# One score run, 64x64 value pieces and a new slot order in a local-attention kernel

## The reference

```python
h = shift_token(x)
q, k, v = split(h @ wqkv)                      # 8 heads of 64
q, k = l2norm(q) * qs, l2norm(k) * ksc
q, k = rotary_xpos(q, k)
sim = einsum('bhwid,bhwjd->bhwij', q * 8, k)   # window 128, keys of this and the previous window
sim = where((i < j) | (i > j + 128) | (j == -1), -max, sim)
out = softmax(sim) @ v
x = x + out @ wo
```

## Time and profile before

| | us |
|---|---|
| median of three runs | 3194.92 |
| lowest, highest | 3190.87, 3195.54 |
| profiled execution, span from first to last instruction | 3193.4 |
| PE busy in it | 3068.6 (96%) |
| DVE, ACT, POOL busy | 2350.6, 1729.0, 1622.9 |

### The profile page before, as it was taken

The page is one execution under the profiler, slowest core; times in us unless marked ns, Lnnn a source line. Parts: engine busy times, 40 slices in busy tenths (PEclk is TensorE's granted clock), DMA queues, the critical chain, the costliest instruction groups (busy, mean ns, idle before and its releaser), DMA issues.

```text
span 3193.4 us, 99022 instructions
## 1 busy us (share of the span) xinstructions
PE 3068.6 (96%) x35586; PEld 2681.3 (84%) x35586; DVE 2350.6 (74%) x6543; ACT 1729.0 (54%) x4532; POOL 1622.9 (51%) x1839
## 2 busy tenths in 40 slices
PE   6999999999999999999899999989999899999889
PEld 5888878878887888998788878878888788888778
DVE  6888767677776787777777767767777688777766
ACT  4767642266767224665667672237767622454445
POOL 7777730177776224333777761037777444317610
PEclk9999999999999999999999999999999999999999
DMA  4211121021111101000211112102111200100001
GB/s 135 67 45 44 37 81 33 23 63 40 36 40 39 42 20 43 11 10 21 58 40 36 40 39 76 30 26 66 37 39 34 72 21 13 27 0 1 1 14 40
DMA packets 178774, 122.82 MB, mean 38 GB/s; under 512 B 27533, under 2 KB 175337, under 8 KB 178025
## 3 DMA queue, kind: packets, MB, share of 16 engines
q1 hardware_dynamic: 177432, 117.77, 13.8%
q10 hardware_dynamic: 1104, 1.90, 0.2%
HBM read 48.29 MB, written 20.98 MB: 22 GB/s over the span
## 4 chain that ended last, share of the span: by engine, by line
PE 87%; DVE 6%; issue 3%; POOL 1%; ACT 1%; DMA 1%; SPq 0%; DVEq 0%; POOLq 0%; ACTq 0%
PE bank L347 15%; PE bank L348 13%; PE bank L349 13%; PE bank L511 8%; PE bank L480 6%; PE bank L452 3%; PE bank L732 2%; PE bank L731 2%; PE bank L730 2%; PE bank L724 2%; PE bank L725 2%; PE bank L489 2%; PE bank L676 2%; PE bank L675 2%; PE bank L490 2%
## 5 line engine op out<-in xcount | busy, mean ns | idle before, releaser
L2652 POOL TENSOR_TENSOR prob<-prob,rsum 128x384 f32<-128x384 f32 x512 | 416.2, 834 | 155.8 <-DVE rsum L1861 155.8
L1209 ACT ACTIVATE prob<-prob,nmax 128x192 f32<-128x192 f32 x1024 | 455.8, 454 | 2.2 <-DVE nmax L1854 2.2
L1401 ACT ACTIVATE gate<-bank,bias 128x512 f32<-128x512 f32 x192 | 132.4, 690 | 512.0 <-PE bank L349 511.9
L2639 POOL TENSOR_TENSOR rn<-ss,mhalf 128x16 f32<-128x16 f32 x128 | 375.9, 2937 | 10.7
L1854 DVE CUSTOM_DVE_ANT_0 prob<-bank,masks,rn 128x192 f32<-128x192 f32 x768 | 275.1, 414 | 100.1 <-PE bank L480 99.3
L2646 POOL TENSOR_TENSOR qk<-rot_t 128x512 f32<-128x512 f32 x256 | 331.9, 1297 | 23.3 <-DVE ss L1828 21.3
L347 PE MATMUL bank<-wqkv_hi,hT_hi 128*128 128x512 f32 x768 | 329.5, 429 | 14.7 <-DVE rot_t L1816 6.1
L2620 POOL TENSOR_TENSOR rstd<-meanvar,eps 128x4 f32<-128x4 f32 x48 | 12.4, 259 | 620.4 <-DVE meanvar L1786 620.4
L348 PE MATMUL bank<-wqkv_lo,hT_hi 128*128 128x512 f32 x768 | 303.0, 395 | 0.0
L349 PE MATMUL bank<-wqkv_hi,hT_lo 128*128 128x512 f32 x768 | 302.8, 394 | 0.0
L347 PE MATMUL bank<-gT_hi,w_hi 128*128 128x512 f32 x704 | 277.2, 394 | 2.6 <-issue 2.6
(11 more groups left out here) (292 smaller groups left out, 9831.1 us busy)
## 6 DMA issues: line engine op xcount, KB each, us to landing
Vlo<-V SPq DMA_DIRECT2D x256, 64.0 KB, 2.0
Vhi<-V SPq DMA_DIRECT2D x256, 64.0 KB, 2.0
H<-Y SPq DMA_DIRECT2D x128, 64.0 KB, 1.8
H<-ya SPq DMA_DIRECT2D x128, 64.0 KB, 1.8
yb<-Y SPq DMA_DIRECT2D x128, 64.0 KB, 1.6
HB<-Y SPq DMA_DIRECT2D x32, 256.0 KB, 2.8
HB<-yb SPq DMA_DIRECT2D x32, 256.0 KB, 3.1
raw<-in_L_ffn_wqkv SPq DMA_DIRECT2D x4, 1536.0 KB, 8.3
```

What stands on the lines that cost most here:

```text
L1209: ins = e.activation(pb, pb, ACT.Exp, bias=nm[r][:, x:x + 1], scale=-1.0, accum_out=sums[r][:, x:x + 1])
L2639: e.tensor_tensor(rn[u][:, :], ss[:, :], mhalf[:, :], ALU.pow).then_inc(s_plRN, 1)
L2652: e.tensor_tensor(pair, pair, rs[:, 2 * gi:2 * gi + 2].unsqueeze(2).to_broadcast([P, 2, KW]), ALU.mult).then_inc(s_plPN[gi], 1)
```

## The change

The banks of PSUM are laid out anew: banks 2 to 4 become one area of 1536 columns in which each head has its 192 columns (SCORE_AT), so that all eight heads' scores of a tile stand there at once; banks 6 and 7 take P times V, heads 0 to 3 in one and 4 to 7 in the other, and the output projection moves to the second half of bank 7. The scores become one run of 32 matmuls with one semaphore at its end, and a wait of PE for a piece of its own in the middle (s_peSB). P times V does the parts with Vlo and Vhi first, with the 64 rows only that belong to the head, as 64x64 pieces, and the parts with V behind them. The turned K and the projected V use bank 5, the turned Q and projected Q bank 0, the turned H and projected K bank 1, the turned P the score banks once they are read. The lists of all four engines are new: the softmax of tile T and its turns (pt_) now lie in slot T, behind its scores. SP's list is the same. The fill (begin) is written out step by step instead of through partial slots, and the drain has one slot less on DVE and ACT.

```diff
+SCORE_AT = (384, 768, 576, 1344, 0, 960, 192, 1152)
+SCORE_ORDER = ((1, 4, 0), (1, 4, 1), (5, 6, 1), (5, 6, 0), (7, 0, 0), (7, 0, 1), (3, 2, 0), (3, 2, 1))
+TURN_BANK = (3, 2, 2, 4)
...
+bank = [ctx.enter_context(nc.psum_tensor(f"bank{i}", [P, 512], F32))[:, :] for i in range(2)]
+scores = ctx.enter_context(nc.psum_tensor("scores", [P, 3 * 512], F32))
+bank += [scores[:, 512 * i:512 * (i + 1)] for i in range(3)]
+bank.append(ctx.enter_context(nc.psum_tensor("bank5", [P, 512], F32))[:, :])
+pair_bank = ctx.enter_context(nc.psum_tensor("pair_bank", [P, 2 * 512], F32))
+bank += [pair_bank[:, 512 * i:512 * (i + 1)] for i in range(2)]
+numerator = pair_bank[:, :].rearrange("p (a c) -> p a c", a=2)[:, :, 0:2 * P]
+projected = bank[7][:, 2 * P:4 * P]
...
+def v_bank(run, T):
+    return bank[0] if run == DEPTH and isinstance(T, int) and T == 0 else bank[5]
+
+def k_turn_bank():
+    return bank[5]
...
         def qk_(T, u, j):
+            early = isinstance(T, int) and T < 3
+            if j == 0 and not early:
+                qT_read(T - 2)
+            elif j == 0 and T == (1 if run == DEPTH else 2):
+                qT_read(0)
+            elif j == 0 and T > 0:
+                q_read(T - 1)
+            elif j == 1 and spare(run, T):
+                k_read(T - 1)
+            proj(bank[j], u, INNER * j, INNER).then_inc(s_peQK[j], 1)
...
         def v_(T, u):
+                if run == DEPTH:
+                    q_read(0)
+            elif isinstance(T, int) and T == 1:
+                kT_read(0)
+            elif isinstance(T, int) and T == 2:
+                v_read(1)
+            else:
+                kT_read(T - 2)
+            proj(v_bank(run, T), u, 2 * INNER, INNER).then_inc(s_peV, 1)
...
         def tr_(T, u, j):
             G = R0 + T
             e.wait_ge(s_plAD[0] if j == 0 else s_dvQN, G + 1 + OFF)
+            if j == 0 and isinstance(T, int) and T == 0 and run == DEPTH:
+                v_read(0)
+            elif j == 0 and inside(T + 1):
+                q_read(T + 1)
+            elif j == 0:
+                qT_read(T - 1)
+            elif isinstance(T, int) and T == 0:
+                v_read(0)
+            elif inside(T + 1):
+                v_read(T + 1)
             else:
+                kT_read(T - 1)
...
+        def sc_(T, u):
             G = R0 + T
             r = u % 2
+            e.wait_ge(s_acKT[0], G + 1 + OFF)
+            e.wait_ge(s_acKT[1], G + 1 + OFF)
+            for g in range(NG):
+                e.wait_ge(s_acPT[g], G + OFF)
             e.sem_inc(s_passed, 1)
+            for n, (odd, even, piece) in enumerate(SCORE_ORDER):
+                if n == 5:
+                    e.wait_ge(s_peSB, G + 1 + OFF)
+                    e.sem_inc(s_passed, 1)
+                for half_ in range(2):
+                    for h in (odd, even):
+                        i = h // 4
+                        m0, l0 = SCORE_AT[h] + DH * i, SCORE_AT[h] + P * (1 - i)
+                        pp = slice(DH * (h % 2), DH * (h % 2) + DH)
+                        c = h // 2
+                        rows = slice(DH * half_, DH * half_ + DH)
+                        queries = qT[r][pp, c * P + DH * half_:c * P + DH * half_ + DH]
+                        if piece == 0:
+                            keys = kT[pp, c, (u - 1 + half_) % U, :]
+                            o = scores[rows, m0:m0 + P]
+                        else:
+                            keys = kT[pp, c, (u - half_) % U, rows]
+                            o = scores[rows, l0:l0 + DH]
+                        opens = piece == 0 and h in (1, 4, 5)
+                        ins = e.matmul(o, queries, keys, start=opens, stop=True, skip_group_check=True)
+                        if half_ == 1 and h == 5 and piece == 1:
+                            ins.then_inc(s_peSB, 1)
+            ins.then_inc(s_peS, 1)
...
         def pt_(T, u, gi):
-            b_ = bank[4 + gi % 2]
+            b_ = bank[TURN_BANK[gi]]
-            e.wait_ge(s_acPT[(gi + 2) % NG], G + gi // 2 + OFF)
+            if gi == 1:
+                e.wait_ge(s_dvMX[2], G + 1 + OFF)
+            if gi == 2:
+                e.wait_ge(s_acPT[1], G + 1 + OFF)
...
+        def pv_(T, u):
             G = R0 + T
+            for g in range(NG):
+                e.wait_ge(s_acPT[g], G + 1 + OFF)
             e.wait_ge(s_acV, G + 1 + OFF)
             e.wait_ge(s_dvOT, G + OFF)
+            if inside(T - 2):
+                y_read(T - 2)
+            e.wait_ge(s_vs[u], 64 * ((G - u) // U + 1) + OFF)
+            e.sem_inc(s_passed, 1)
             before_ = (u - 1) % U
+            keys = (V[before_], V[u], Vleft[u % 2][0], Vleft[1 - u % 2][1])
+
+            def product(gi, i, x, rows, start):
+                h = PAIRS[gi][i]
+                cols = slice(DH * (h % 2), DH * (h % 2) + DH)
+                o0 = (h // 2 % 2) * P + DH * (x % 2)
+                p0 = (i if x < 2 else 2) * P + DH * (x % 2)
+                return e.matmul(bank[6 + i][cols, o0:o0 + DH], keys[x][rows, h * DH:(h + 1) * DH], PTs[gi][rows, p0:p0 + DH], start=start, stop=x < 2, skip_group_check=True)
+            for hf in range(2):
+                for x in (2, 3):
                     for g in range(2):
+                        for i in range(2):
+                            product(2 * hf + g, i, x, slice(DH * i, DH * i + DH), hf == 0 and x == 2)
+            for hf in range(2):
+                for i in range(2):
+                    for x in (0, 1):
+                        for g in range(2):
+                            ins = product(2 * hf + g, i, x, slice(0, P), False)
+                ins.then_inc(s_pePV[hf], 1)
...
# TensorE
         def slot(T, u):
+            if inside(T):
+                sc_(T, u)
             if inside(T - 1):
+                pv_(T - 1, (u - 1) % U)
             if inside(T - 2):
                 wo_(T - 2, (u - 2) % U)
             if inside(T + 1):
                 tr_(T + 1, (u + 1) % U, 0)
+            if inside(T + 2):
+                v_(T + 2, (u + 2) % U)
+            if inside(T + 3):
+                ht(T + 3, (u + 3) % U)
+            if inside(T):
+                pt_(T, u, 1)
+                pt_(T, u, 0)
+            if inside(T + 1):
+                tr_(T + 1, (u + 1) % U, 1)
+            if inside(T + 3):
+                qk_(T + 3, (u + 3) % U, 0)
+            if inside(T):
+                pt_(T, u, 3)
+                pt_(T, u, 2)
+            if inside(T + 3):
+                qk_(T + 3, (u + 3) % U, 1)
...
# ScalarE
         def slot(T, u):
+            if inside(T + 2):
+                qk_(T + 2, (u + 2) % U, 1)
+            if inside(T):
+                sc_(T, u, 1)
+                sc_(T, u, 0)
+                sc_(T, u, 3)
+                sc_(T, u, 2)
+            if inside(T - 1):
+                ot_(T - 1, (u - 1) % U)
             if inside(T + 1):
+                tr_(T + 1, (u + 1) % U, 0)
+            if inside(T + 2):
+                v_(T + 2, (u + 2) % U)
+            if inside(T + 3):
+                ht(T + 3, (u + 3) % U)
             if inside(T):
+                pt_(T, u, 1)
+                pt_(T, u, 0)
             if inside(T + 1):
+                tr_(T + 1, (u + 1) % U, 1)
+            if inside(T + 3):
+                qk_(T + 3, (u + 3) % U, 0)
             if inside(T):
+                pt_(T, u, 3)
+                pt_(T, u, 2)
...
# VectorE
-            if last and u == U - 1:
+            if last and u == U - 2:
-            if run == 0 and u == U - 1 and not (isinstance(it, int) and it > GRP - 4):
+            if run == 0 and u == U - 2 and not (isinstance(it, int) and it > GRP - 4):
         def slot(T, u):
+            if inside(T + 2):
+                sum_(T + 2, (u + 2) % U, 0)
+            if inside(T):
+                sc_(T, u, 1)
+                sc_(T, u, 0)
+                sc_(T, u, 3)
+                sc_(T, u, 2)
+                rs_(T, u, 0)
             if inside(T + 2):
                 qk_(T + 2, (u + 2) % U, 1)
+            if inside(T):
+                rs_(T, u, 1)
+            if inside(T + 1):
+                norm_(T + 1, (u + 1) % U, 1)
+            if inside(T + 3):
                 ht(T + 3, (u + 3) % U)
             if inside(T + 2):
                 sum_(T + 2, (u + 2) % U, 1)
             if inside(T - 1):
+                ot_(T - 1, (u - 1) % U)
             if inside(T - 2):
+                wo_(T - 2, (u - 2) % U)
+            if inside(T + 3):
+                qk_(T + 3, (u + 3) % U, 0)
...
# GpSimd
         def slot(T, u):
             if inside(T + 1):
+                add_(T + 1, (u + 1) % U, 1)
+            if inside(T + 2):
+                add_(T + 2, (u + 2) % U, 0)
+            if inside(T):
+                pn_(T, u, 1)
+                pn_(T, u, 0)
+                pn_(T, u, 3)
+                pn_(T, u, 2)
+            if inside(T + 2):
+                pow_(T + 2, (u + 2) % U)
...
# VectorE, end of a pass
@@ -1973,18 +2017,21 @@
         if run == 0:
```

(76 more changed lines are left out.)

254 lines of the change are left out of this document (60 added, 194 removed).

## The result

The changed kernel takes 3218.05 us (median of four runs, 3212.2 to 3219.04) where the kernel before takes 3195.23 in the same comparison: ratio 1.0072, 95% interval 1.0057 to 1.0086. It is slower by 0.7%. The forecast was 3202, the range 3168 to 3238. The profiled execution spans 3216.0 us, 22.6 more than that of before.

What follows compares the result with a forecast made beforehand. PE, 96% busy, bounds the kernel before; a ring through PE, DVE and ACT of some 12.40 us per slot replaces it. Passes +3.5, self-wait +2.5, first pass +4, third -3: together +7, 3202 us, range 3168 to 3238.

Steps and rivals of the forecast that it cites:

- The ring: Steady slot, scores to next scores through PE, DVE and ACT: some 12.40 us, PE standing still some 1.1.
- PE's own work: PE's work per slot, from one score run and 64x64 pieces: falls from 12.21 to 11.2 us (11.13 to 11.8).
- the passages that gave way: P times V's entry (0.14) and the score run's exit (0.22) become one change from 64x64 to 128x64, taken at 0.2.
- The ring's size: Sum of slot terms: 12.39 us, plus a quarter of 0.11 for a fourth DVE wait, some 12.40.
- The self-wait: PE's wait inside the score run for its own piece: 0.02 us per slot, 128 x 0.02 = +2.5.
- The ends and the first pass: Second pass: head 54.8, tail 18.3, sum 415.9 (+0.9); first pass: layer norm on DVE +1 to +7, taken +4.
- the slow spell: Behind the second pass's 3.27 us wait a turn took 0.47, not 0.27; may go and return behind H(3)'s wait.
- The third pass: Start of that pass: POOL's normalisation stands behind five other tasks, which the new order shortens: -3 us.
- A shorter ring: Slots: a term overlaps, so at 12.1 us the time is 3168; chance 0.25 including PE-bound, 0.20 near 3175.
- PE as the bound: Slots: V always in time, slot 11.25 us, time 3085; chance 0.05.
- Rival 3: DVE's K scaling falls behind POOL normalisation: ring 13.3 in every second slot, +52 us, time 3255; chance 0.15.
- Rival 4: 64x64 pieces do not run four at a time; PE reaches K turn 0.5 later, time unchanged; chance 0.15.

Runs made afterwards that it cites:

- o_copy_last: Changed kernel with ACT's O copy of tile T-1 moved behind the hT_hi copy of T+3: 3163.59 us, ratio 0.9896.
- scores_wait_last: Changed kernel with DVE waiting for the scores last, not first, of its waits ahead of the reductions: 3181.68 us, ratio 0.9956.
- split_run: Changed kernel with PE's four turns of Q(T+1) put in the middle of the score run, cutting it in two: 3305.35 us, ratio 1.0344.

## Why the prediction was right, and where it was not

**The bound changed as said.** The ring replaces PE as the bound; o_copy_last, scores_wait_last and split_run each change one term of it and the slot moves by that term (0.48, 0.23, 0.75). From start to start the K turn comes 0.72 late (0.7 said; the trace calls 0.56 of it idle, since the turn ahead is drawn 0.27 long), the Q projection 0.28 (0.4 said).

**PE's own work** fell from 12.21 to about 11.3 (12.31 less these two delays) where 11.2 was said: one run saves 0.31 instead of 0.36, the pieces 0.36 instead of 0.48, and what is left of the 0.91, some 0.24, is the passages that gave way (0.16 said). Of the size that was said, and without effect, as said.

**The ring's size: two errors that cancel.** A normal slot is 12.31 and not 12.39: hT_lo to PE took 0.06, with the K turn drawn right up to the Q projection, not the 0.15 of a start from idle. Every fourth slot costs 0.41 more, not 0.11: the term that was mis-sized. The wait itself was priced rightly. In the loop DVE's sequencer also works out three register values in that slot, one each ahead of its second, third and fourth wait, and for these the step had nothing. The last group of four of each pass stands outside the loop, with the fourth wait and without the register steps, and shows the two apart. Second pass, tiles 24 (in the loop, scores at 957.35) and 28 (outside, scores at 1007.04); then one of the register steps over the whole execution:

```profile
959.79 0.42 DVE L1893 CUSTOM_DVE_ANT_0 prob<-scores,mask,rn 128x192 f32<-128x192 f32 x1 [1.40 <-PE scores L508]
...
1009.19 0.42 DVE L1893 CUSTOM_DVE_ANT_0 prob<-scores,mask,rn 128x192 f32<-128x192 f32 x1 [1.02 <-PE scores L508]
```

```profile
L1886 DVEq FUSED_REGOPS  x22: 94/99/99, 92.6 to 2456.4; - x22
```

DVE starts 2.44 behind the first score in the one and 2.15 in the other, where slots with three waits have 2.03: 0.12 for the wait, 0.29 for the register steps. Together 12.41 for the 12.40 foretold, and that the two errors cancel is luck.

**The self-wait** of the score run was to cost 0.02 a slot; the run takes 1.57, the ring's term without it was 1.56. Nothing to see: 2.5 us too many.

**The ends and the first pass.** The second pass grew by 2.9 (+1.5 said, self-wait included): its head took 57.6 (54.8 said), the part between the scores of tile 3 and the last scores 343.3 (342.8), the tail 17.0 (18.3). The fourth grew by 3.15 (+1.5). The first grew by 5.6 (+5.5), but by another split: the slots with layer norm take 1.9 more in four slots where 0.5 to 1.6 was said, so that layer norm costs, net of what it cost before, some 7 us and not 4, and the tail gives 5.8 back, not 4.6. The wait for H(3) is 2.6 as said (2.9). What the prediction left open, the slow spell, came behind this wait in the second pass:

```profile
664.00:667.00 3.00, 1.42 (x11) 1.21 (x12) 2.42 (x6) 2.90 (x10) 2.87 (x4) 1.00 0.01 3
667.00:670.60 3.60, 3.60 (x14) 2.92 (x13) 0.59 (x2) 1.25 (x3) 3.09 (x3) 0.53 0.02 5
```

After stops of 2.62 and 0.80 us PE is granted 0.53 of the full clock in this window (0.50 from 667.2 to 670.5), the level of 1.2 GHz instead of 2.4, and a projection matmul takes 0.43 instead of 0.23: some 1.5 us. The drain of the second pass, where the kernel before had its spell (0.50 from 1035.1 to 1041.8), is at full clock. In the fourth pass it is the other way round; its head, then its tail:

```profile
2137.46:2193.54 56.08, 45.39 (x516) 35.56 (x514) 40.39 (x116) 33.40 (x94) 43.98 (x37) 1.00 0.13 32
2536.90:2556.21 19.31, 15.52 (x249) 13.35 (x249) 12.51 (x37) 9.26 (x28) 4.32 (x6) 0.82 0.10 22
```

The tail at 0.82 takes 19.31, 2.3 us more than the 17.04 of the second pass at full clock.

**The third pass** is the step that failed: -3 was said, because a wait of 4.7 us ahead of the first turns of P would shrink. It went, and a wait of 4.3 for the rotary step of K(2), which DVE does behind the reductions of the first tile, took its place; with the stop of 3.24 and slow spells at its end (its tail is 20.0, where the second pass has 17.0) the pass is +7.0 where -1.5 was said. Outside the passes nothing was counted, and it is +3.9; 3.1 of that go with the other stop. So of the 15.6 us between the 7 foretold and the 22.6 measured, some 6 go with the two stops that moved with the code, some 5.5 are the third pass besides, and some 3 the second and fourth pass.

**The rivals.** A shorter ring (3168) did not come by itself; with two orders changed it did, with a span of 3150. PE as the bound (3085) came in no run. Rival 3, the K scaling behind POOL: it takes 692 ns in the middle of 128 and 1591 at most, so it did not come. Rival 4 is refuted: eight instructions of the 64x64 pieces come in 0.12 us, 0.015 each (884.48 to 884.61), as said for four at once, where the 128x64 form takes 0.034.

## What to carry to other kernels

Before the work of the busiest engine is cut, walk the new order from one fixed point of a slot to the same point of the next through all engines: if that ring is as long as the slot, only its own terms count, whoever is 96% busy. Then look in the ring for things nobody on it waits for: a copy placed before a needed one (0.48 us a slot here) and a late wait placed ahead of early ones (0.23 to 0.65). Behind a ring that has been shortened look for the next one, from start to start and not by busy shares. And judge a part of a change in an order in which it lies on the bound: the 64x64 pieces were worth nothing in one order, 24 us in a second, 32 in a third.

## What the hardware showed that was not expected

- A satisfied wait costs DVE about 0.11 us, and the three register steps that go with the waits of every fourth slot 0.29 together. Eight satisfied waits hold PE 0.24 to 0.78 ahead of the score run (0 to 0.08 without them) and 0.02 to 0.31 behind it.
- Single stops of 2 to 4 us of PE move with the code's position; the two of the changed kernel make some 6 us of its 22.6.
- PE can be drawn busy in 282.73 of 284.45 us and still wait 0.29 in every slot.
- Of four layer-norm scalings beside POOL's addition one took 1.36 us instead of 0.41; beside POOL's power none did.
